# Keys of an image pair without zero rows, score products on 64 rows each, and TensorE's attention chunk loop written out

## The reference, cut to what matters

```
# L0, for feat = groupnorm(x), per image
feat_value = l2norm_over_channels(W @ feat + b)        # 64 x 3136
f          = l2norm_over_channels(feat)                # 64 x 3136, keys and queries
attention  = clip(einsum('ncp,ncq->npq', f, f), 0)**2  # 3136 x 3136
out        = einsum('ncq,npq->ncp', feat_value, attention)
# L1 and L3 gather 4 corners at 9 taps of each pixel; L2 is a recurrence over diagonals
```

## Time and profile before

| What | us |
|---|---|
| median of 3 runs (14364.51 to 14372.98) | 14365.74 |
| the profiled execution's own time | 14491.91 |
| its span, first to last instruction | 14489.8 |
| round 0 (attention alone), chunks | 119 to 574 |
| rounds 1 to 7 | 574 to 6354 |
| last round (sampling, skewing) | 6354 to 7136 |
| recurrence and L3 | the rest |

### The profile page before, as it was taken

The page is one execution under the profiler, slowest core; times in us unless marked ns, Lnnn a source line. Parts: engine busy times, 40 slices in busy tenths (PEclk is TensorE's granted clock), DMA queues, the critical chain, the costliest instruction groups (busy, mean ns, idle before and its releaser), DMA issues. The chain is left out here.

```text
span 14489.8 us, 110898 instructions
## 1 busy us (share of the span) xinstructions
PE 8644.1 (60%) x26294; PEld 3625.3 (25%) x26294; DVE 6885.5 (48%) x8889; ACT 4883.7 (34%) x7671; POOL 8632.6 (60%) x7465
## 2 busy tenths in 40 slices
PE   7888887878788787852188888233332323333322
PEld 2333333323233333321044444111111111111111
DVE  3444545454544545444344444444454454444444
ACT  4444443434344444431178888111111111111100
POOL 0176775757576675767500000477777777777777
PEclk9899898989899898975599999555555555555555
DMA  0122222222222222227522222634343443433332
GB/s 7 37 84 78 87 82 82 82 81 82 81 82 81 83 84 80 85 84 175 139 56 56 58 56 56 127 98 115 97 114 101 114 114 99 115 98 98 97 94 88
DMA packets 1168915, 1277.68 MB, mean 88 GB/s; under 512 B 795967, under 2 KB 924415, under 8 KB 1164671
## 3 DMA queue, kind: packets, MB, share of 16 engines
q0 software_dynamic: 338688, 925.30, 21.6%
q1 hardware_dynamic: 815710, 347.84, 10.5%
q10 hardware_dynamic: 14368, 3.21, 0.1%
HBM read 1080.00 MB, written 195.82 MB: 88 GB/s over the span
## 5 line engine op out<-in xcount | busy, mean ns | idle before, releaser
L423 POOL DMA_INDIRECT b_gathered<-table,b_iu x3528 | 4451.0, 1262 | 1323.9 <-issue 988.5
L423 POOL DMA_INDIRECT d_gathered<-table,d_iu x3528 | 4114.3, 1166 | 1279.1 <-issue 1049.6
L518 PE MATMUL PS<-b_key 128*128 (+1 forms) x5600 | 2557.9, 583 | 18.2 <-ACT b_weights L694 7.3
L543 PE MATMUL PS<-ident,d_sample 128*128 128x128 f32 (+1 forms) x1960 | 504.2, 421 | 3229.5 <-DVE d_sample L893 2996.5
L694 ACT ACTIVATE b_weights<-PS 128x896 f32<-128x896 f32 (+1 forms) x1400 | 1281.8, 916 | 2296.3 <-PE PS L518 1886.3
L531 PE MATMUL PS<-b_weights,b_values 128*64 128x448 f32 (+1 forms) x5600 | 1466.7, 591 | 619.0 <-DVE b_weights L873 585.0
L881 DVE TENSOR_TENSOR d_gathered<-d_gathered,d_w 128x2304 f32<-128x2304 f32 x392 | 1002.6, 2558 | 1494.8 <-DMA d_gathered<-table,d_iu 1451.8
L881 DVE TENSOR_TENSOR b_gathered<-b_gathered,b_w 128x2304 f32<-128x2304 f32 x392 | 1002.2, 2557 | 1395.2 <-DMA b_gathered<-table,b_iu 1391.5
L704 ACT ACTIVATE d_sampleT<-PS 128x512 f32<-128x512 f32 x392 | 233.2, 595 | 3346.0 <-PE PS L543 2676.3
L518 PEld LDWEIGHTS PS<-b_key 128*128 128x128 f32 (+1 forms) x5600 | 994.5, 197 | 1330.5 <-issue 1325.1
L873 DVE TENSOR_TENSOR b_weights<-b_weights 128x896 f32<-128x896 f32 x672 | 731.2, 1088 | 1185.2 <-ACT b_weights L694 943.3
(11 more groups left out here) (224 smaller groups left out, 9533.6 us busy)
## 6 DMA issues: line engine op xcount, KB each, us to landing
b_gathered<-table,b_iu POOLq DMA_INDIRECT x3528
d_gathered<-table,d_iu POOLq DMA_INDIRECT x3528
l_x_and_h<-xs SPq DMA_DIRECT2D x224, 224.0 KB, 3.6
hs<-l_hT SPq DMA_DIRECT2D x224, 224.0 KB, 2.4
d_h<-hs SPq DMA_DIRECT2D x32, 1554.0 KB
table<-b_table_rows SPq DMA_DIRECT2D x208, 128.0 KB, 1.9
table<-d_table_rows SPq DMA_DIRECT2D x208, 128.0 KB
xs<-b_key SPq DMA_DIRECT2D x14, 1568.0 KB
```

What stands on the lines that cost most here:

```text
L423: pool.indirect_dma_start(GB[:, g, k, :], None, tables[b], bass.IndirectOffsetOnAxis(ap=ix, axis=0)).then_inc(gathered[g], 16)
L518: mm = pe.matmul(PS[0:keys(k), 2 * (k % S_BUFS) + a, 0:CH], KEY[:, a, k * P:k * P + keys(k)], KEY[:, a, bass.ds(j * CH, CH)], start=True, ...
L543: mm = pe.transpose(PS[0:n, 5 + s // 4, (s % 4) * P:(s % 4 + 1) * P], S[:, t % 2, s * P:s * P + n], K.ident[:, :])
```

## The change

`KEY` keeps its shape, but both images' keys now stand in half 0, image 0 in partitions 0 to 63 and image 1 in 64 to 127; no part of it is zeroed and the two memsets go, with their count. A score product reads only the 64 partitions of its image. And where a round has attention, PE's chunk loop is written out in Python (7 copies of the chunk in PE's program, in round 0 and again within the hardware loop over i); the last round keeps its hardware loop. The loops of other engines stay.

```diff
-        ZEROED = 3 + NB + (3 if att else 0)
+        ZEROED = 3 + NB + (1 if att else 0)
...
                 wait_apart(pe, relu_done, c * QT + 1 + max(k - 1, 0))
                 for a in (0, 1):
-                    mm = pe.matmul(PS[0:keys(k), 2 * (k % S_BUFS) + a, 0:CH], KEY[:, a, k * P:k * P + keys(k)],
-                                   KEY[:, a, bass.ds(j * CH, CH)], start=True, stop=True)
+                    r = slice(a * C, (a + 1) * C)
+                    mm = pe.matmul(PS[0:keys(k), 2 * (k % S_BUFS) + a, 0:CH], KEY[r, 0, k * P:k * P + keys(k)],
+                                   KEY[r, 0, j * CH:(j + 1) * CH], start=True, stop=True)
                 mm.then_inc(scores_ready, 1)
...
-                with pe.Fori(0, NCH) as j:
-                    if i is None:
+                if i is None:
+                    with pe.Fori(0, NCH) as j:
                         sampling_chunk(m, b, q, None, j, False)
-                    else:
+                else:
+                    for j in range(NCH):
                         scores(i * NCH + j, j, 0)
...
-            if att:
-                v.memset(KEY[C:P, 0, :], 0.0).then_inc(zeroed, 1)
-                v.memset(KEY[0:C, 1, :], 0.0).then_inc(zeroed, 1)
...
-                        v.tensor_tensor(KEY[r, a, px], G[r, px], RLEN[r, 0, :], ALU.mult)
+                        v.tensor_tensor(KEY[r, 0, px], G[r, px], RLEN[r, 0, :], ALU.mult)
```

## The result

The changed kernel takes 14251.0 us (14248.65 to 14252.45, 3 runs) against 14365.74: ratio 0.9919, 95% interval 0.9896 to 0.9941. Forecast were 14258 us and a range of 14215 to 14362. The profiled execution took 14251.0 us as well.

A forecast was written before the change was run, and what follows sets the result against it. PE was taken to bound round 0 and POOL's gathers rounds 1 to 7. From the profiled 14491.91 us, -122 - 6.8 + 21 = -108 gave 14384, and 126 lower for the median 14258 us; range 14215 to 14362.

The forecast's parts named there:

- The bound of each stretch: PE bounds round 0; POOL's gathers bound rounds 1 to 7, at 103.7 us a chunk against PE's 85.
- Part 1, the step: Score products side by side: a block's scores and values go from 2.60 to 1.85 us, round 0 gains 122 us.
- Rival (a): Two products on 64 rows do not run side by side, only the memsets count: 14359 us, chance 11%.
- the estimate of 1.17 us: Score group of a block if two tiles reach only 77%: 0.53 us less a step, about -87 us in round 0.
- head and end: Round 0's chunk: values(0) starts 1.66 us earlier at the head; 0.7 us charged at the end, where values(24) waits.
- ACT's floor: ACT's relu and square in round 0 take 1.35 us a block, under PE's new step of 1.85.
- Part 2: At the start, without the two memsets, the load of `gp` and all behind it move up: -6.8 us.
- Part 3: PE's chunk loop written out: 0 us, with bounds of 0 to 28 us for exposed instruction fetches.
- Rounds 1 to 7: Nothing gained in the chunks; the tail behind the last gather loses 3 us a round to PE's lower clock, +21 us.
- rival (b): Tail and next preparation run at 1.2 GHz: 23 us a round lost, 14421 us, slower from 16 a round; chance 6%.
- The bound of -20 us for round 1: A faster PE may remove POOL's waits for samples in round 1: -20 to 0 us, taken as 0.
- the poorer tail: Named with the 77% tiles and the fetches as what takes the forecast's own range up to 14320 us.

The follow-up runs named there:

- both doublings: The changed kernel with each score product issued twice: in round 0 alone 14374.0 us, in rounds 1 to 7 alone 14204.6 us.
- the six gathers: Six gathers per tile instead of nine where rounds have attention: in the kernel before 13425.4 us, in the changed kernel 12740.2 us.
- the squares on ACT: The changed kernel with the squares of odd blocks moved from DVE to ACT: 13994.9 us, ratio 0.9733.
- the second profile of before: The kernel before, run and profiled again with no edit: 14369.7 us, profiled span 14369.8 us.
- the first profile: The profile of the kernel before that the prediction was made from, with no edit: 14491.91 us, against a median of 14365.74.

## Why the prediction was right, point by point

**The bound of each stretch**: right, by both doublings (+123 in round 0, no cost in rounds 1 to 7) and by the six gathers. One reading under it does not hold: the last round's 101.4 us a chunk was taken for POOL's pace without attention, so that removing all attention would buy 2.3 us a chunk. With the squares on ACT the rounds with attention run at (522.4 + 163.7) / 7 = 98.0 us, below that. The last round has other work of DVE, and is no measure of POOL alone.

**Part 1, the step**: 2.60 to 1.85 us was forecast and is measured; the two images' products stand side by side. Rival (a) is out. The 77% of a four-tile figure on the Trainium skill's page TensorE: Matmul & The Clock Gate (section Part 3: Packing small matmuls), which the estimate of 1.17 us used, is not seen for two tiles of 64 rows: 0.95. One whole chunk: 17.5 was forecast, 17.8 measured. 17.8 less 22 x 0.75 leaves 1.3 for head and end together, where I had 1.0. Over seven chunks 124.7 against 122. ACT's floor did not bind in the steps; only the head waits for it.

**Part 2**: -6.8 forecast, 6.75 between first loads, 6.3 by the run with the memsets back, 6.9 by its first load.

**Part 3**: nothing forecast, nothing measured.

**Rounds 1 to 7**: +21 forecast, +16.4 measured, and here the mechanism was half wrong. I put +3 us a round into the tail behind the last gather, for the clock. The tail got 1.6 us shorter, although it does begin at the lower clock, for it began so in the second profile of before as well (1.62 us for the values at 2188.32); I had taken the tail at full clock from the first. The loss by the clock is in the next preparation (offsets, +1.7, where it shows), a place that I had given to rival (b) alone. And the largest part, +2.9, is in the gathers, which I had held constant. The step that failed is "POOL's 103.7 stays, its order and DVE's are the same: 0 in the chunks". The order did stay, and the gathers still took 2.9 us longer; by inference, they lie differently beside DVE's work. That three terms add up to about what I forecast for one of them is luck. The bound of -20 us for round 1 came from the first profile as well, where POOL waited 19.9 us for samples in that round; in the second it waited 0.9.

**From profile to median**: I took the 126 us between them for the profiler's. It was not: the profiled executions of the change and of before again are within 2 us of their medians. It did no harm, since all terms were differences. It would have, had I compared the first profile with the one after: that shows rounds 6.7 us shorter, a gain that does not exist. POOL's lead of 116.9 us at the last round accounts for nearly all of the 120.7 between the second profile's span and the change's; 3.8 lie behind it, in stages that the change does not touch.

**The range**: its own terms give 14258 - 20 - 21 = 14217 and 14258 + 35 + 28 = 14321, so the upper end of 14320 has no room left for the poorer tail that it names. It decides nothing here.

Rival (b), with its point of decision at 16 us a round, saw 2.2 of its 23.

**Still open**: why the gathers are shorter with the doubled products in rounds 1 to 7, and most from round 4 on. That gathers depend on what DVE runs beside them is shown by the squares; that the 2.9 us, and the 46 us of the doubling, have this cause is inferred from that, and from there being nothing else on POOL.

## What to carry to other kernels

An engine at 70% busy may be the bound: what shows it is that no other engine is named in its waits, and, more surely, that doubling the busier engine's work costs nothing. A stage without that work is only a hint, since it may have other work in its place. Before you credit a change with a small gain per round, compare a stage that it does not touch, or profile the kernel before a second time. When a product contracts over zeros, halve its rows and let two run side by side; but shorten the bounding engine first, since here the same edit was worth 115 us behind nine gathers and 685 behind six.

## What the runs showed of the hardware

Two products on 64 rows each (partitions 0 to 63 and 64 to 127, different banks) take the time of one: eight MATMULs of 448 columns in 1.70 us at 2.4 GHz, four in 0.95 with the turns.

A gather takes 0.94 us of POOL at its shortest, and is stretched beside an instruction of DVE with two inputs. Timelines of POOL and DVE, changed kernel, round 3:

```profile
2164.37 0.95 POOL L423 DMA_INDIRECT b_gathered<-table,b_iu  x1 [0.31 <-issue]
2165.62 0.94 POOL L423 DMA_INDIRECT b_gathered<-table,b_iu  x1 [0.30 <-issue]
...
2179.58 2.80 POOL L423 DMA_INDIRECT b_gathered<-table,b_iu  x1 [0.30 <-issue]
```
```profile
2162.04 5.75 DVE L862 RECIPROCAL b_weights<-b_weights 128x896 f32<-128x896 f32 x1
...
2179.02 2.55 DVE L880 TENSOR_TENSOR b_gathered<-b_gathered,b_w 128x2304 f32<-128x2304 f32 x1
```

Beside the reciprocal, with one input, gathers keep their 0.95 us; beside the product of 2.55 us one takes 2.80. The stretch is not the same each time: beside the short products of `keys_and_values` (two in 1.25 us, then one of 0.62) the gather at 2178.11 takes 1.17 us. Moving 84 squares of 1.09 us a round (92 us) off DVE shortened POOL's gathers by 31, about 0.34 us for each us of squares. The Trainium skill (GPSIMD Engine Reference, section Specifications) says that GpSimd shares its SBUF interfaces with VectorE and that DVE instructions with two SBUF inputs contend with it; the trace agrees.
